# Masked attention, one core: 2304 instead of 2048 of a tile's 4096 columns turned by DMA

## What is computed

```python
q = x @ Wq.T + bq;  k = x @ Wk.T + bk;  v = x @ Wv.T + bv     # x: 4096 x 128, f32
scores = q @ k.T / sqrt(128)
scores = where(adj > 0, scores, -9e15)                        # adj: 4096 x 4096, int32
att = softmax(scores, axis=-1) @ v
y = x + elu(att)
out = (y - mean(y)) / sqrt(var(y) + 1e-5)                     # per row
```

## Time and profile before

| | |
|---|---|
| median of 3 runs | 437.78 us (437.71 to 438.47) |
| the profiled execution: its time, its span | 437.62 us, 435.8 us |
| busy share of the span | PE 97%, DVE 83%, ACT 82%, POOL 79% |
| DMA, mean | 240 GB/s, 104.76 MB |
| granted TensorE clock, mean | 0.998 of full speed |

### The profile page before, as it was taken

The page is one execution under the profiler, slowest core; times in us unless marked ns, Lnnn a source line. Parts: engine busy times, 40 slices in busy tenths (PEclk is TensorE's granted clock), DMA queues, the critical chain, the costliest instruction groups (busy, mean ns, idle before and its releaser), DMA issues.

```text
span 435.8 us, 11399 instructions
## 1 busy us (share of the span) xinstructions
PE 424.1 (97%) x3479; PEld 311.0 (71%) x3479; DVE 362.5 (83%) x671; ACT 355.5 (82%) x736; POOL 343.9 (79%) x613
## 2 busy tenths in 40 slices
PE   8998999999999999999999999999999999999984
PEld 6663677677777777777777777777777777777783
DVE  0768988888898988888898988888889888888764
ACT  4778787888888988888888988888888988888982
POOL 0064558898889888898889888898889888898864
PEclk9999999999999999999999999999999999999999
DMA  8922999999999999999999999999999999998550
GB/s 222 380 98 97 188 267 263 266 254 290 268 271 280 250 256 281 259 256 258 271 272 265 254 247 276 269 260 250 268 272 265 259 249 272 264 266 206 102 105 18
DMA packets 149932, 104.76 MB, mean 240 GB/s; under 512 B 133024, under 2 KB 141728, under 8 KB 141728
## 3 DMA queue, kind: packets, MB, share of 16 engines
q1 hardware_dynamic: 149488, 104.41, 90.4%
q10 hardware_dynamic: 432, 0.20, 0.2%
HBM read 69.47 MB, written 2.10 MB: 164 GB/s over the span
## 4 chain that ended last, share of the span: by engine, by line
POOL 58%; issue 18%; PE 11%; DMA 3%; SPq 3%; DVE 3%; POOLq 2%; ACT 2%; ACTq 0%; DVEq 0%
POOL p_rows L317 26%; POOL res L331 6%; POOL rstd L355 4%; POOL neg_mean L342 3%; DMA p_turned<-p_rows 3%; POOL y L336 3%; POOL att_sum L324 3%; POOL var L351 3%; POOL att L326 3%; SPq L258 3%; POOL centred L344 2%; POOL expm L333 2%; POOL var_eps L353 2%; PE ps_t L711 2%; POOL y_out L359 2%
## 5 line engine op out<-in xcount | busy, mean ns | idle before, releaser
L317 POOL TENSOR_TENSOR p_rows<-scores,p_rows 128x256 f16<-128x256 f32 x252 | 175.9, 729 | 12.2 <-ACT p_rows L463 12.2
L582 DVE CUSTOM_DVE_ANT_0 scores<-ps_scores,adj 128x1024 f32<-128x1024 f32 x128 | 156.0, 1219 | 14.5 <-issue 10.9
L446 ACT ACTIVATE scores<-scores,neg_max 128x1024 f32<-128x1024 f32 x128 | 145.6, 1138 | 0.5 <-DVE neg_max L591 0.5
L597 DVE TENSOR_TENSOR p_lo<-ps_t,p_hi 128x512 f16<-128x512 f32 x124 | 82.5, 685 | 27.5 <-ACT p_hi L455 27.1
L568 DVE TENSOR_SCALAR adj<-adj 128x1024 f32<-128x1024 int32 x128 | 104.2, 814 | 0.7 <-DMA adj<-in_adj_dram 0.6
L767 PE MATMUL ps_scores<-k_hi,q_hi 128*128 128x512 f16 x256 | 97.1, 379 | 1.0 <-DVE max_parts L582 0.9
L768 PE MATMUL ps_scores<-k_lo,q_hi 128*128 128x512 f16 x256 | 97.0, 379 | 0.0
L769 PE MATMUL ps_scores<-k_hi,q_lo 128*128 128x512 f16 x256 | 97.0, 379 | 0.0
L806 PE MATMUL ps_out<-v_parts,p_turned 128*128 128x256 f16 x496 | 95.1, 273 | 1.0 <-DMA p_turned<-p_rows 0.8
L806 PE MATMUL ps_out<-v_parts,p_hi 128*128 128x256 f16 x496 | 95.3, 273 | 0.8 <-DVE p_lo L597 0.5
L808 PE MATMUL ps_out<-v_parts,p_lo 128*128 128x128 f16 x496 | 88.5, 219 | 0.0
(11 more groups left out here) (89 smaller groups left out, 474.8 us busy)
## 6 DMA issues: line engine op xcount, KB each, us to landing
adj<-in_adj_dram SPq DMA_DIRECT2D x64, 1024.0 KB, 5.3
out_dram<-y_out SPq DMA_DIRECT2D x32, 64.0 KB, 4.8
x_rows<-in_x_dram SPq DMA_DIRECT2D x4, 256.0 KB, 4.2
x_rows<-in_x_dram SPq DMA_DIRECT2D x2, 512.0 KB, 6.1
p_turned<-p_rows SPq DMA_TRANSPOSE x63, 4.5
w_rows<-in_L_gnn_Wk_dram ACTq DMA_DIRECT2D x1, 64.0 KB, 2.6
w_rows<-in_L_gnn_Wq_dram ACTq DMA_DIRECT2D x1, 64.0 KB, 3.3
w_rows<-in_L_gnn_Wv_dram ACTq DMA_DIRECT2D x1, 64.0 KB, 4.0
```

The source lines that it names most:

```text
L317: last = nc.gpsimd.tensor_tensor(p_rows[c][:, w:][:, cols], s_sb[s][:, c * PIECE:c * PIECE + w][:, cols], p_rows[c][:, 0:w][:, cols], ALU. ...
L446: nc.scalar.activation(s_sb[s][:, cols], s_sb[s][:, cols], ACT.Exp, bias=neg_max[:, s:s + 1], accum_out=p_sums[:, s, c:c + 1]).then_inc(ex ...
L582: nc.vector.tensor_tensor_reduce(out=s_sb[s][:, cols], in0=ps_scores[c % 2][:, :], in1=mask_sb[s][:, cols], scale=SCALE, scalar=-3.0e38, o ...
L597: nc.vector.tensor_tensor(p_lo[:, k, :], ps_t[bank_of(s, g)][:, :], p_hi[:, k, :], ALU.subtract).then_inc(plo_ready, 1)
```

## The change

The split between the two ways moves by 256 columns: the second DMA transpose takes columns 1024 to 2303. Group 4 (columns 2048 to 2559) is now mixed: its first two blocks come by DMA, its other two by PE. With it:
- PE makes two transposes for group 4 instead of four. ACT's and DVE's parts of group 4 have 256 columns instead of 512. ACT's `high_rows` of piece 1 has 1280 columns instead of 1024, waits for exponentials up to piece 2, and POOL's `low_rows` of piece 1 has five instructions of 256 columns instead of four. T1 moves 1280 columns of both parts.
- The values of group 4 are in two parts; the part by DMA comes last in the period. `T_AT` and `PV_ORDER` are new: group 5 is turned in step 6 (was 7), group 7 in step 1 of the next period (was 2).
- SP issues both halves of the adjacency rows of tile p+1 back to back behind T1, with nothing behind T0.
- DVE makes the masks of pieces 1, 2, 3 of the running tile in steps 1, 3, 5 and piece 0 of the next in step 7; before it was piece 3 of the running tile in step 1 and pieces 0, 1, 2 of the next in steps 3, 5, 7. One mask stands ahead of period 0 instead of three.

```diff
-DMA_COLS = (PIECE, PIECE)
+MIXED_COLS = 256
+DMA_COLS = (PIECE, PIECE + MIXED_COLS)
+MIXED = FIRST_PE
-T_AT = {4: 6, 5: 7, 6: 8, 7: 10}
-PV_ORDER = (4, 5, 6, 0, 1, 7, 2, 3)
+T_AT = {4: 6, 5: 6, 6: 8, 7: 9}
+PV_STEPS = ((5,), (4,), (6,), (7, 0), (1,), (2,), (3,), (TURNED_HALF,))
-LOW_PARTS = 4
+LOW_COLS = 256
...
+        def by_pe(g):
+
+            return slice(MIXED_COLS, BANK) if g == MIXED else slice(0, BANK)
...
                 if turns_1:
                     turn(p - 2, n, 1)
-                if head:
+                if loads:
+                    load_half(p + 1, 1 - n, 0, False)
                     load_half(p + 1, 1 - n, 1, False)
                 if stores:
                     store(p - 4, n)
                 if turns_0:
                     turn(p - 1, 1 - n, 0)
-                if loads:
-                    load_half(p + 2, n, 0, False)
...
-                for b in range(LOW_PARTS):
+                for b in range(w // LOW_COLS):
...
-                act.wait_ge(exp_done, exp_count(i, c))
+                act.wait_ge(exp_done, exp_count(i, (c * PIECE + w - 1) // PIECE))
...
-                    if j == 1 and has_scores:
-                        mask_piece(p, n, 3)
-                    if j in (3, 5, 7) and has_scores and makes_mask:
-                        mask_piece(p + 1, 1 - n, j // 2 - 1)
+                    if j in (1, 3, 5) and has_scores:
+                        mask_piece(p, n, j // 2 + 1)
+                    if j == 7 and has_scores and makes_mask:
+                        mask_piece(p + 1, 1 - n, 0)
...
-                for b in range(BLOCKS):
+                for b in range(by_pe(g).start // P, BLOCKS):
                     kb = g * BLOCKS + b
                     last = nc.tensor.transpose(ps_t[bank][:, b * P:(b + 1) * P], s_sb[s][:, kb * P:(kb + 1) * P], ident[:, :])
```

More of the change, by code:

```diff
@@ L20 @@
 LOG_P_SCALE = 15.0 * math.log(2.0)
-DMA_COLS = (PIECE, PIECE)
+MIXED_COLS = 256
+DMA_COLS = (PIECE, PIECE + MIXED_COLS)
 BY_DMA = len(DMA_COLS)
 FIRST_PE = sum(DMA_COLS) // BANK
+MIXED = FIRST_PE
 PE_GROUPS = STEPS - FIRST_PE
-T_AT = {4: 6, 5: 7, 6: 8, 7: 10}
-PV_ORDER = (4, 5, 6, 0, 1, 7, 2, 3)
+T_AT = {4: 6, 5: 6, 6: 8, 7: 9}
+TURNED_HALF = STEPS
+PV_STEPS = ((5,), (4,), (6,), (7, 0), (1,), (2,), (3,), (TURNED_HALF,))
+PV_ORDER = tuple(g for step in PV_STEPS for g in step)
+PV_PARTS = len(PV_ORDER)
 POOL_OPS = 11
-LOW_PARTS = 4
+LOW_COLS = 256
 LAST_OPS = 9
@@ L258, in turn, with period @@
                 sp.dma_start_transpose(p_turned[c][s][:, :, :], p_rows[c][:, :]).then_inc(turned[c], 16)
-            def period(p, n, head=True, turns_0=True, turns_1=True, stores=True, loads=True):
+            def period(p, n, turns_0=True, turns_1=True, stores=True, loads=True):
                 if turns_1:
                     turn(p - 2, n, 1)
-                if head:
+                if loads:
+                    load_half(p + 1, 1 - n, 0, False)
                     load_half(p + 1, 1 - n, 1, False)
@@ L269, in period @@
                     turn(p - 1, 1 - n, 0)
-                if loads:
-                    load_half(p + 2, n, 0, False)
             load(0, 0)
             load(1, 1)
-            period(0, 0, head=False, turns_0=False, turns_1=False, stores=False)
             period(1, 1, turns_1=False, stores=False)
@@ L281, in _ @@
                     period(2 * pair + n, n)
-            period(TILES - 2, 0, loads=False)
-            period(TILES - 1, 1, head=False, loads=False)
+            period(TILES - 2, 0)
+            period(TILES - 1, 1, loads=False)
             turn(LAST - 1, 0, 1)
@@ L574, in masked_piece @@
                 if not first:
[L575 to L576 removed]
+                    if 2 * c <= MIXED:
+                        dve.wait_ge(rows_lo, BY_DMA * (i - 2) + min(c + 1, BY_DMA))
                     if 2 * c + 1 >= FIRST_PE:
@@ L784, in transposes, with values @@
                 last.then_inc(pt_ready, 1)
-            def values(i, s, g, first):
-                if g >= FIRST_PE:
+            def values(i, s, part, first):
+                g = MIXED if part == TURNED_HALF else part
+                by_dma = part < FIRST_PE or part == TURNED_HALF
+                c = min(g // 2, BY_DMA - 1)
+                if not by_dma:
                     pe.wait_ge(plo_ready, PE_GROUPS * i + g - FIRST_PE + 1)
-                elif g % 2 == 0 or pv_count(0, g - 1) > pv_count(0, g):
-                    pe.wait_ge(turned[g // 2], 16 * i + 16)
-                if g == PV_ORDER[0] and not first:
+                elif part % 2 == 0:
+                    pe.wait_ge(turned[c], 16 * i + 16)
+                if part == PV_ORDER[0] and not first:
                     pe.wait_ge(att_ready, i - 1)
@@ L796, in values @@
                     pe.wait_ge(v_lo, STEPS)
-                for b in range(BLOCKS):
+                turned_blocks = by_pe(g).start // P
+                blocks = range(turned_blocks) if part == TURNED_HALF else range(turned_blocks, BLOCKS)
+                for b in blocks:
                     k = g * BLOCKS + b
-                    if g >= FIRST_PE:
+                    if by_dma:
+                        high = p_turned[c][s][:, k - c * PIECE // P, :]
+                        low = p_turned[c][s][:, DMA_COLS[c] // P + k - c * PIECE // P, :]
+                    else:
                         high = p_hi[:, g - FIRST_PE, b * P:(b + 1) * P]
                         low = p_lo[:, g - FIRST_PE, b * P:(b + 1) * P]
-                    else:
-                        high = p_turned[g // 2][s][:, g % 2 * BLOCKS + b, :]
-                        low = p_turned[g // 2][s][:, DMA_COLS[g // 2] // P + g % 2 * BLOCKS + b, :]
                     nc.tensor.matmul(ps_out[s][:, 0:2 * D], high, v_parts[:, k, :],
-                                     start=(g == PV_ORDER[0] and b == 0), stop=False)
+                                     start=(part == PV_ORDER[0] and b == blocks[0]), stop=False)
                     last = nc.tensor.matmul(ps_out[s][:, D:2 * D], low, v_parts[:, k, D:2 * D],
-                                            start=False, stop=(g == PV_ORDER[-1] and b == BLOCKS - 1))
+                                            start=False, stop=(part == PV_ORDER[-1] and b == blocks[-1]))
                 last.then_inc(pv_done, 1)
@@ L851, in period @@
                             transposes(p - 1, 1 - n, g, not warm)
-                    if has_2:
-                        values(p - 2, n, PV_ORDER[j], first)
+                    for g in PV_STEPS[j]:
+                        if has_2:
+                            values(p - 2, n, g, first)
             period(0, 0, has_1=False, has_2=False, warm=False)
@@ L865, in _ @@
             transposes(LAST - 1, 0, 6, False)
-            values(LAST - 1, 0, 4, False)
+            values(LAST - 1, 0, 5, False)
             transposes(LAST - 1, 0, 7, False)
-            for g in (0, 1, 5, 6, 2, 7, 3):
-                values(LAST - 1, 0, g, False)
+            for part in (4, 0, 1, 6, 7, 2, 3, TURNED_HALF):
+                values(LAST - 1, 0, part, False)
             for g in range(LAST_PE, STEPS):
```

24 lines of the change are left out of this document (10 added, 14 removed).

## The result

| | before | after |
|---|---|---|
| median | 437.75 us (437.66 to 438.47) | 449.47 us (449.27 to 450.38, 4 runs) |
| the profiled execution: its time, its span | 437.62, 435.8 us | 449.31, 447.5 us |
| mean time between two `att_sum`, over 25 | 12.23 us | 12.65 us |
| granted TensorE clock, mean | 0.998 | 0.998 |

The changed kernel is slower: ratio 1.027, 95% interval [1.0261, 1.0286], 11.7 us where 8.4 were forecast.

The account below looks back on a forecast made before the run. The prediction took PE to set the pace, POOL 0.34 us a period behind, and POOL's list to lead after the change: 437.62 + 7.5 (25 periods) + 0.9 (end) = 446.0 us, range 433 to 453.

Parts of the forecast that it names:

- POOL's list overtakes PE: Steady periods: POOL's list would need 12.53 us a period, more than PE's 12.01; chance 0.64.
- POOL's room: POOL's wait for ACT's att, less a dependent start: about 0.34 us in a period of 12.23.
- The fifth instruction costs 0.64 us: POOL's low rows of piece 1: one more instruction a period adds 0.64 us if no mask stands in its way.
- The other bound: POOL's fifth instruction with a DVE mask on it: 0.44 us more, 12.97 a period and 457.0 us.
- POOL's list takes 12.53: POOL's period: 12.23 - 0.34 + 0.64 us, with masks paid as before and no wait for att.
- rival 1: DVE masks fall into POOL's row-sum wait, POOL needs 12.14 or less, PE's pace is reached: 430.8 us; chance 0.17.
- POOL busy about 364 us: Sign in the changed kernel's profile: POOL's busy time, 343.9 + 31 x 0.64 us, from the added instructions alone.
- The start 0: Start up to the early periods: fewer transposes, masks made later, taken as 0, within 1 us.
- The end +0.9: End of the kernel: later low rows 0.64, longer T1 0.72, shorter PE work -0.4, together +0.9 us.
- Rival 4: T0 queued behind two loads on DMA delays ACT's high rows: 12.37 us a period, 454.5 in all with 12.87; chance 0.09.
- Rival 2: ACT and POOL's loop through att and y, with group 7's high part ahead, takes 12.25 us: 438.5 us; chance 0.10.
- DVE has room: DVE: the low part of group 4 is halved, so no cost was taken for DVE.

Follow-up runs that it names:

- e9: Changed kernel with the values of group 7 back in step 5, behind scores 4 and 5, instead of step 3: 448.77 us.
- e1: Kernel before plus a fifth 256-column low-part instruction on POOL, writing to a spare buffer, nothing else changed: 444.89 us.
- e4: Kernel before with only the new T_AT table (group 5 turned in step 6, group 7 in step 1 of the next period): 438.90 us.
- e10: Changed kernel with the values of group 7 in step 5 and without POOL's fifth low-part instruction: 439.96 us.
- e2: Changed kernel without POOL's fifth low-part instruction (low part of columns 2048 to 2303 left zero): 448.59 us.
- e11: Changed kernel with group 7's values in step 5, ACT's high rows of piece 1 ahead of row_sum, and negative mean from ACT's row sum: 439.50 us.
- e3: Kernel before with only the changed kernel's order of loads on SP and places of DVE's masks: 437.41 us.
- e8: Changed kernel with loads and masks put back in the order of the kernel before: 450.75 us.

## Why the prediction was right, and where its sizes were off

- *POOL's list overtakes PE, although PE is busy 97% before.* Right: e9 shows POOL's list alone at 12.62 us, and PE's saved transposes show nowhere in the time. But PE has a part in the second loop, which I had not seen.
- *POOL's room is 0.34 us a period.* Near: e1 takes 0.64 us more work and grows by 12.48 - 12.23 = 0.25, so the room was 0.39, as far as the masks hit as before.
- *The fifth instruction costs 0.64 us, no mask on it.* Right: 3.20 us for five. The other bound, 0.44 more, didn't come.
- *So POOL's list takes 12.53.* Low by 0.09: 12.62. The prediction said that POOL pays for each mask as before and has no wait but the row sum. Both halves were wrong, with opposite signs. One mask fell into a wait and spared POOL 0.38 us, much as rival 1 had it, though with the new wait and not that for the row sum. (Rival 1's 12.14 should read 12.53 - 0.38 = 12.15; nothing hangs on it.) But I had looked only at whether ACT's sum of work changed, not at who waits for the 0.22 us by which its high rows grew; there were 0.13 us of cover, and POOL now waits 0.49 us there. 24 x 0.09 = 2.2 us of the 3.3 by which 446.0 fell short of 449.31; the rest is the start (0.8) and the one long period (0.8), less 0.5 for the end.
- *POOL busy about 364 us.* Wrong for the changed kernel (355.4), right for e1 (364.5), which has the same instructions: the 9 us between them are masks that hit POOL less, `centred` above all (12.4 us in all its 31 instances against 21.2 in e1).
- *The start 0.* +0.8, in the periods ahead of 100.20. *The end +0.9.* +0.4: the longer T1 landed in 4.87 us, not in 5.11 and 0.72 more. This is the chain of waits near the end (answers to rows 6), start us, us:

```profile
427.13 4.87 DMA p_turned<-p_rows
432.05 0.28 PE ps_out L816
433.88 1.33 PE ps_scores L828 x12
```

  Behind it PE takes 433.88 - 432.05 = 1.83 us instead of 2.16: 0.33 less, 0.4 was forecast.
- *Rival 4, T0 late.* Once: the period of 13.35 us, 0.7 over the others, where ACT's high rows wait for T0 (ACT's timeline of the changed kernel):

```profile
101.20 1.06 ACT L470 ACTIVATE p_rows<-scores 128x1024 f16<-128x1024 f32 x1 [0.82 <-DMA p_turned<-p_rows]
```

- *Rival 2.* Not decided. e4 and e10 run at 12.30 us with ACT and POOL waiting for each other, near the 12.25 worked out, but 0.52 us of that is a wait for PE, so ACT and POOL alone are not what holds it.
- *What I did not see: PE and DVE.* The prediction costs the moved values and transposes at nothing and says that DVE has room. That holds for its sum of work. It does not hold for the way from PE's scores through DVE to the low part that PE wants ahead of its next scores, 3.7 + 9.0 us. The step that sent it there was the place of group 7's values in the new `PV_ORDER`, which the prediction did not follow through DVE. Had POOL been cheaper, the time would still have been 448.6 (e2). That the forecast was near in spite of it is luck: the loop that I had not seen happened to be no longer than the one that I had costed. And the trace of after, by the chain alone, would have told me that I was entirely right.

The sum again, with what was measured: 437.62 + 0.8 + 24 x (12.62 - 12.23) + (13.35 - 12.23) + 0.4 = 449.3.

## What to carry to other kernels

Where engines work in a pipeline that is full, count loops, not engines: write down for each pair that waits for each other once a period what lies on the way round, and do it anew for every table of steps that is changed, also for engines with room. When a cost is confirmed by a trace, take it out and see whether the time comes back; if it does not, look for a second loop of the same length, for then single edits each look worthless until both are made. A worked-out length that comes near the measured one does not yet name the loop: see that no wait for a third engine lies in it (e10). An instruction that grows on an engine with idle time must be checked against the one behind it in another queue: cover is the gap between its end and its reader's start, here 0.13 us, not the engine's idle share.

## What the runs showed of the hardware

- A DVE mask (128 x 1024, int32 to float32) that starts just before an instruction of POOL stretches it: `res` 0.45 to 0.90 us, `att` 0.46 to 0.90, `neg_mean`, a 128 x 1 operation, 0.19 to 0.57. The one that starts beside `centred` at 221.08 in the changed kernel and lasts through POOL's wait costs POOL nothing; it takes 0.88 us itself, where the same mask took 0.69 before. So the same number of instructions kept POOL busy for 355.4 us in the changed kernel and 364.5 in e1. The Trainium skill (SBUF — State Buffer, "Who interferes with whom") has the two engines share a port pair as an exclusive lock; these rows agree that POOL is held, for 0.38 to 0.45 us by a mask of some 0.7 us.
- Which instructions the masks hit depends on how POOL and DVE lie against each other: the same list on POOL, 613 instructions, is busy for 343.9 us before and for 326.6 in e4, where only the steps of the transposes moved. In e11, where POOL had been relieved, four instructions a period were stretched, in the changed kernel three. So the gain of a shorter POOL cannot be read from the instruction's length alone.
- Two loads of 1 MB back to back land 7.0 to 7.2 us after issue in the median instead of 5.3 to 5.4 apart (in e3 and the changed kernel against e8 and before). The transposes beside them hardly feel it: 4.7 us in e3 instead of 4.5 before, and 4.9 in the changed kernel as in e8.
